# Fused attention and feed-forward layer on one core: slots of queries and keys copied on chip, and the last block's finish in halves with precedence

## The reference

```python
Q, K = apply_rope(Q), apply_rope(K)
attn = einsum('bqhd,bkhd->bhqk', Q, K) * head_dim ** -0.5      # causal mask, softmax
x = x + (attn @ V) @ w_proj + b_proj                           # on layernorm(x)
real = layernorm(x) @ cos(theta + theta_noise)
imag = layernorm(x) @ sin(phi + phi_noise)
x = x + sqrt(real * real + imag * imag)
```

## Time and profile before

| | |
|---|---|
| median of three runs | 2075.5 us (2075.34 to 2077.35) |
| the profiled execution | 2075.44 us, its span 2073.7 us, so 1.7 us lie outside the span |
| TensorE busy | 98% of the span |
| VectorE, ScalarE, GpSimd busy | 72%, 68%, 42% |
| mean granted TensorE clock | 0.992 of full speed |

### The profile page before, as it was taken

How to read it: one execution, slowest core, us unless ns; L and a number is a source line. 1 busy time by engine, 2 the same in 40 slices (tenths; PEclk the granted TensorE clock), 3 DMA queues, 4 the chain that set the end, 5 groups by cost and what they waited for, 6 DMA issues and landing times.

```text
span 2073.7 us, 39127 instructions
## 1 busy us (share of the span) xinstructions
PE 2028.7 (98%) x13124; PEld 877.2 (42%) x13124; DVE 1493.0 (72%) x2724; ACT 1403.4 (68%) x2705; POOL 871.7 (42%) x1336
## 2 busy tenths in 40 slices
PE   7999999999999999999999999999999999999988
PEld 5333343344443444444443444434444344433335
DVE  4858878877768777786767768787676877678423
ACT  2455667777667666776667676687666767677673
POOL 3334426353433435544263453447343353630252
PEclk9999999999999999999999999999999999999999
DMA  5322322232222322232222212333222232320031
GB/s 144 80 47 86 88 62 78 78 95 72 72 74 61 90 77 73 88 95 73 66 86 80 81 58 65 95 97 88 78 62 76 66 95 77 89 80 17 28 123 44
DMA packets 120552, 159.90 MB, mean 77 GB/s; under 512 B 30746, under 2 KB 82586, under 8 KB 120346
## 3 DMA queue, kind: packets, MB, share of 16 engines
q1 hardware_dynamic: 118480, 154.18, 25.4%
q10 hardware_dynamic: 1872, 3.21, 0.8%
HBM read 88.89 MB, written 50.85 MB: 67 GB/s over the span
## 4 chain that ended last, share of the span: by engine, by line
PE 83%; ACT 6%; issue 3%; DMA 3%; POOL 2%; DVE 2%; SPq 1%; ACTq 0%; DVEq 0%; POOLq 0%
PE banks L938 21%; PE banks L916 21%; PE banks L953 20%; PE banks L871 5%; PE banks L882 5%; ACT probs L1049 3%; PE banks L914 3%; PE banks L898 3%; PE banks L834 2%; DVE chunk_max L1195 1%; ACT inverse L1069 1%; ACT xin L1062 1%; PE banks L823 1%; DMA stack_k<-split 1%; POOL guess L1272 1%
## 5 line engine op out<-in xcount | busy, mean ns | idle before, releaser
L1195 DVE TENSOR_REDUCE chunk_max<-banks 128x1 f32<-128x512 f32 (+3 forms) x2240 | 1350.4, 667 | 393.6 <-PE banks L916 389.3
L1049 ACT ACTIVATE probs<-banks 128x512 f32<-128x512 f32 (+1 forms) x2240 | 1141.3, 601 | 384.7 <-PE banks L938 302.3
L916 PE MATMUL banks<-stack_k,stack_q 96*128 96x512 bf16 (+3 forms) x2560 | 730.5, 351 | 4.9 <-DVE chunk_max L1195 2.1
L938 PE MATMUL banks<-stack_q,stack_k 99*128 99x512 bf16 (+3 forms) x2560 | 695.1, 350 | 11.7 <-ACT probs L1049 9.2
L953 PE MATMUL banks<-probs,v_one 128*17 128x512 f32 (+3 forms) x5120 | 527.7, 532 | 4.2 <-POOL probs L1337 3.1
L938 PEld LDWEIGHTS banks<-stack_q,stack_k 99*128 99x128 bf16 x2560 | 231.9, 97 | 393.8 <-ACT probs L1049 206.4
L916 PEld LDWEIGHTS banks<-stack_k,stack_q 96*128 96x128 bf16 x2560 | 239.8, 98 | 240.4 <-DVE chunk_max L1195 75.7
L1337 POOL TENSOR_SCALAR_AFFINE_SELECT probs<-probs 128x512 f32<-128x512 f32 x256 | 160.7, 638 | 220.0 <-ACT probs L1049 219.5
L953 PEld LDWEIGHTS banks<-probs,v_one 128*17 128x17 f32 x5120 | 119.0, 96 | 288.6 <-issue 192.2
L914 PE MATMUL banks<-diag_mask,ident_bf 128*128 128x128 bf16 x1024 | 200.7, 223 | 6.2 <-DMA stack_k<-split 4.4
L587 POOL TENSOR_TENSOR turned<-raw,cos_t 128x512 f32<-128x512 f32 x62 | 78.9, 1273 | 290.7 <-ACT raw L1011 287.6
(11 more groups left out here) (134 smaller groups left out, 1181.2 us busy)
## 6 DMA issues: line engine op xcount, KB each, us to landing
split<-parts SPq DMA_DIRECT2D x64, 384.0 KB, 2.7
stack_q<-split SPq DMA_DIRECT2D x384, 64.0 KB, 2.2
stack_k<-split SPq DMA_DIRECT2D x354, 64.0 KB, 2.2
sums<-o_raw SPq DMA_DIRECT2D x64, 256.0 KB, 2.2
rot<-raw SPq DMA_DIRECT2D x246, 64.0 KB, 2.0
xin<-x SPq DMA_DIRECT2D x16, 512.0 KB, 4.0
heads_t<-sums SPq DMA_DIRECT2D x26, 256.0 KB
mid<-x SPq DMA_DIRECT2D x13, 512.0 KB, 4.0
```

What stands on the lines that cost most here:

```text
L916: mm = nc.tensor.matmul(bank[:, n * wide:(n + 1) * wide], stack_q[u % 2][0:SPLIT_ROWS, t, h + n, j * P:(j + 1) * P], stack_k[u % 2][0:SPLI ...
L938: mm = nc.tensor.matmul(bank[:, a * wide:(a + 1) * wide], stack_k[u % 2][0:ROWS, j // SUB, first + a, (j % SUB) * P:(j % SUB + 1) * P], st ...
L1049: nc.scalar.activation(probs[:, g % PROBS, first:first + many, w0:SPAN], bank, ACT.Exp).then_inc(s_exp, 1)
L1195: nc.vector.tensor_reduce(to, bank[:, 0:count * wide].rearrange("p (h n) -> p h n", h=count), AX.X, ALU.max).then_inc(s_emptied["DVE"], 1)
```

## The change

Three things are changed, and one number with them.

1. **Slots are read from `parts`.** `keep`, the DRAM tensor `split` and its semaphore go. Each slot copy reads 64 partitions of `parts`, 1 KB of each, where it read 16 rows of 4 KB from DRAM. `fetch` and `fetch_k` wait for the last rope instruction, and rope instruction 3, which writes `parts`, waits for the slots of two spans before (it waited for their `keep`; the `keep` itself waited for those slots).
2. **The last block.** `spread`, the reciprocal over a whole bank and the multiplication on `o_raw` give way to `apart` (four transposes that bring rows to partitions), a reciprocal of 16 numbers a partition, a multiplication out of the bank, `together` (four transposes back) and a copy. Its stats, deviation, apply and `xt3` go in halves. Every job of it has the due time `LAST_AT` = 15.4, ahead of the finishes of blocks 13 and 14.
3. **Block 14** has its power, modulus, add and final in halves too (`IN_HALVES`), on VectorE and ScalarE where GpSimd did them.
4. **Numbers of the plan:** `apply` 2.1 for 1.35 us, `exp` 0.02 us longer, the scores of the last span due 0.1 of a unit earlier.

```diff
 FINAL = BLOCKS - 1
+
+IN_HALVES = (FINAL - 1, FINAL)
+LAST_AT = 15.4
+LAST_PULL = 0.1
 SETS = SPANS
...
+
+    def halved(n, a, at):
+        job(("power", n, a), "DVE", 0.7, at, [("out", ("wave", n, 2 * a + 1))])
+        job(("modulus", n, a), "ACT", 0.6, at, [("power", n, a), ("modulus", n, a - 1)])
+        job(("add", n, a), "DVE", 0.7, at, [("modulus", n, a)])
+        job(("final", n, a), "SP", 0.4, at, [("add", n, a), ("final", n, a - 1)], 3.0)
...
         unit = GROUPS * b + GROUPS - 1
-        todo.append((GROUPS * (b + 1) + t + 0.1 if b < BATCH - 1 else ends(unit, t) + 0.05, "finish", n, 0))
+        todo.append((GROUPS * (b + 1) + t + 0.1 if b < BATCH - 1 else LAST_AT if n == FINAL else ends(unit, t) + 0.05, "finish", n, 0))
...
-            job(("apply", n), "ACT", 1.35, at, [("dev", n)])
+            job(("apply", n), "ACT", 2.1, at, [("dev", n)])
...
-                after += [("keep", *ago)] if n == 3 else []
+                after += [("fetch", *ago), ("fetch_k", *ago)] if n == 3 else []
...
-            job(("keep", u, c), "SP", 0.45, at, [("rope", u, c, ROPE_OPS - 1), ("fetch", *ago), ("fetch_k", *ago)], 2.4)
             if i < HELP:
-                job(("fetch_k", u, c), "ACT", 3.6, at, [("keep", u, c)], 2.2)
-            job(("fetch", u, c), "SP", 2.7 if i < HELP else 5.4, at, [("keep", u, c), ("scores", LAST_STEP.get(u - 2), 0)], 2.2)
+                job(("fetch_k", u, c), "ACT", 3.6, at, [("rope", u, c, ROPE_OPS - 1)], 2.2)
+            job(("fetch", u, c), "SP", 2.7 if i < HELP else 5.4, at, [("rope", u, c, ROPE_OPS - 1), ("scores", LAST_STEP.get(u - 2), 0)], 2.2)
...
-                job(("spread",), "PE", 0.85, at, [("lift", unit, t), ("lead", n, 1), ("weights",)])
-                with_bank(("spread",), ("spread",), "DVE", 3.6, at)
-                job(("divide",), "DVE", 0.7, at, [("out", ("spread",))])
+
+                at = LAST_AT
+                job(("apart",), "PE", 0.44, at, [("lift", unit, t), ("weights",)])
+                with_bank(("apart",), ("apart",), "DVE", 0.85, at)
+                job(("together",), "PE", 0.44, at, [("out", ("apart",))])
+                with_bank(("together",), ("together",), "DVE", 0.65, at)
                 for a in range(2):
...
+                    job(("proj", n, a), "PE", 0.9, at, [("out", ("together",)), ("lead", n, 1), ("proj", n, a - 1)])
+                    with_bank(("proj", n, a), ("proj", n, a), "DVE", 0.65, at, [("out", ("lead", n, a))])
+                    job(("stats3", n, a), "DVE", 1.0, at, [("out", ("proj", n, a)), ("stats3", n, a - 1)])
+                    job(("dev3", n, a), "POOL", 2.8, at, [("stats3", n, a), ("dev3", n, a - 1)])
+                    job(("apply3", n, a), "ACT", 1.05, at, [("dev3", n, a)])
+                    job(("xt3", n, a), "PE", 0.44, at, [("apply3", n, a), ("xt3", n, a - 1)])
+                    with_bank(("xt3", n, a), ("xt3", n, a), "ACT", 0.55, at)
+                    for j in (2 * a, 2 * a + 1):
+                        job(("wave", n, j), "PE", 4 * KT * 2 * DIM / 2400, at, [("out", ("xt3", n, a)), ("wave", n, j - 1)])
+                        with_bank(("wave", n, j), ("wave", n, j), "ACT", 0.6, at, [("power", n, 0)] if j > 1 else [])
+                    halved(n, a, at)
...
-                    job(("exp", g, n), "ACT", 0.06 + many * wide / 1200, at, [("scores", g, n), prev, ("values", g4 - g4 % VALUES)])
+                    job(("exp", g, n), "ACT", 0.08 + many * wide / 1200, at, [("scores", g, n), prev, ("values", g4 - g4 % VALUES)])
```

The addresses of the slot copies, the waits, and the new products:

```diff
-                    engine.wait_ge(s_keep[i % 2], 16 * (i // 2))
+                    engine.wait_ge(s_fetch[i % 2], LOADS * (i // 2))
...
             tile = (stack_q, stack_k)[side][u % 2][slot * HD:(slot + 1) * HD, c, :, :]
-            rows = split[PLACE[u, c] % 2, part, side * P // 2:(side + 1) * P // 2, :]
-            return tile.rearrange("p h n -> p (h n)"), rows.rearrange("(d h) n -> d (h n)", h=HG)
+            rows = parts[side * P // 2:(side + 1) * P // 2, PLACE[u, c] % 2, part, :]
+            return tile, rows
...
-                def keep_parts(u, c):
+                def fetch_slots(u, c):
                     i = PLACE[u, c]
                     sp.wait_ge(s_rope, ROPE_OPS * (i + 1))
-                    if i >= 2:
-                        sp.wait_ge(s_fetch[i % 2], LOADS * (i // 2))
-                    sp.dma_start(split[i % 2].rearrange("m r n -> r m n"), parts[:, i % 2, :, :]).then_inc(s_keep[i % 2], 16)
-
-                def fetch_slots(u, c):
-                    i = PLACE[u, c]
-                    sp.wait_ge(s_keep[i % 2], 16 * (i // 2 + 1))
                     if u >= 2:
                         sp.wait_ge(s_scores, FILLS[LAST_STEP[u - 2] + 1])
...
-                def spread_denominators():
+                def turn_sums():
                     u, t = SCORED[-1]
                     pe.wait_ge(s_lift, len(SCORED))
-                    pe.wait_ge(s_last_weights, 32)
-                    bank = bank_of(("spread",))
-                    nc.tensor.matmul(bank, spread, o_raw[:, TURN[u, t] % 2, :], start=True, stop=True).then_inc(s_filled["DVE"], 1)
+                    bank = bank_of(("apart",))
+                    for j in range(SUB):
+                        mm = nc.tensor.transpose(bank[:, j * P:(j + 1) * P], o_raw[:, TURN[u, t] % 2, j * P:(j + 1) * P], ident[:, :])
+                    mm.then_inc(s_filled["DVE"], 1)
+
+                def turn_back():
+                    emptied(pe, ("apart",))
+                    bank = bank_of(("together",))
+                    for j in range(SUB):
+                        mm = nc.tensor.transpose(bank[:, j * P:(j + 1) * P], last_rows[:, j * P:(j + 1) * P], ident[:, :])
+                    mm.then_inc(s_filled["DVE"], 1)
+
+                def turn_last(a):
+                    pe.wait_ge(s_last_norm, a + 1)
+                    bank = bank_of(("xt3", FINAL, a))
+                    for k in range(KT):
+                        for j in range(2):
+                            at = (2 * k + j) * P
+                            mm = nc.tensor.transpose(bank[:, at:at + P], normed3[finish_set(FINAL)][:, 2 * a + j, k * P:(k + 1) * P], ident[:, :])
+                    mm.then_inc(s_filled["ACT"], 1)
...
-                    pe.wait_ge(s_divided, 1)
+                    emptied(pe, ("together",))
+                    pe.wait_ge(s_last_weights, 16)
                     bank = bank_of(("proj", FINAL, a))
```

VectorE's part of it, and its norm statistics in halves (the new functions `deviation_last` and `normalise_last` do the same eight and two instructions on half of the columns):

```diff
+                def block_stats_last(a):
+                    emptied(dve, ("proj", FINAL, a))
+                    for j in (2 * a, 2 * a + 1):
+                        nc.vector.bn_stats(last_stats[:, j, :], mid[finish_set(FINAL)][:, j, :]).then_inc(s_last_stat, 1)
+                    dve.wait_ge(s_last_stat, 4 * a + 2)
+                    for j in (2 * a, 2 * a + 1):
+                        nc.vector.bn_aggr(last_mv[:, j, :], last_stats[:, j, :]).then_inc(s_last_stat, 1)
...
-                    if item[0] == "spread":
+                    if item[0] == "apart":
                         dve.wait_ge(s_rope, ROPE_OPS * len(PROJECTED))
-                        nc.vector.reciprocal(crossed[:, :], bank).then_inc(s_emptied["DVE"], 1)
+                        sums_of = bank.rearrange("p (j h v) -> p j h v", h=HG, v=VW)
+                        nc.vector.reciprocal(last_inverse, sums_of[:, :, :, HD]).then_inc(s_last_inverse, 1)
+                        dve.wait_ge(s_last_inverse, 1)
+                        inverse = last_inverse.unsqueeze(3).to_broadcast([P, SUB, HG, VW])
+                        nc.vector.tensor_tensor(last_rows.rearrange("p (j h v) -> p j h v", h=HG, v=VW), sums_of, inverse,
+                                                ALU.mult).then_inc(s_emptied["DVE"], 1)
+                        return
+                    if item[0] == "together":
+                        nc.vector.tensor_copy(last_heads[:, :], bank).then_inc(s_emptied["DVE"], 1)
```

More of the change, by code:

```diff
@@ L211, in plan @@
         job(("tables", c), "SP", 0.9, CLOCK[0, c - 1] - 1.05, [("rot", 0, c - 1)], 5.0)
-    job(("wv",), "SP", 0.8, -0.7, [("keep", 0, 0)], 3.0)
+    job(("wv",), "SP", 0.8, -0.7, [("rope", 0, 0, ROPE_OPS - 1)], 3.0)
     job(("wqk",), "SP", 0.5, -0.3, [("fetch", 0, 2)], 3.0)
@@ L513, in layer_kernel @@
         late_wproj = wqk[:, 0, :, :].rearrange("p k n -> p (k n)")
-        spread = wqk[:, 1, 0, :]
         last_heads = turned
+        last_rows = raw[:, 0, :]
+        small = iter(crossed[:, n * 4 * SUB:(n + 1) * 4 * SUB] for n in range(9))
+        last_stats = crossed[:, 256:256 + 6 * SUB].rearrange("p (j s) -> p j s", s=6)
+        last_inverse = next(small).rearrange("p (j h) -> p j h", h=HG)
+        last_mv = next(small)[:, 0:2 * SUB].rearrange("p (j s) -> p j s", s=2)
+        last_variance, last_centre, last_guess, last_correction, last_rstd, last_shift = (next(small)[:, 0:SUB] for _ in range(6))
         out_bank = psum[RING]
@@ L550, in layer_kernel @@
         s_rope = sem("rope_chain")
```

(28 more changed lines are left out.)

135 lines of the change are left out of this document (70 added, 65 removed).

## The result

The changed kernel takes 2051.07 us (median of 4 runs, 2046.19 to 2051.54) against 2075.42 of before in the same comparison: ratio 0.9876, 95% interval 0.9859 to 0.9893. The profiled execution took 2051.54 us, with a span of 2049.4.

A forecast was written before the change was run, and what follows sets the result against it. TensorE, busy 98% of the span, was taken as the bound, except at the opening and the end. From 2075.4 us, opening -4, body +4 and end -9.2 gave 2066.2 us, range 2056 to 2074.5.

The forecast's parts named there:

- The opening: Start of the kernel: earlier slots and new order of unit 0 gain 4 us, from a loss of 4 to a gain of 10.
- The second span: Opening: its slots, issued at about 36.4, reach TensorE at 44.5 to 45.4 against 49.82, a gain of 5 us.
- The third step, the hole: Opening, unit 0's order: VectorE's 16 us hole moves forward between maxima of spans 2 and 3, TensorE having about 16 us work.
- The slots' own price: Slot copies in 1 KB pieces out of SBUF: priced at nothing, at worst four times the time.
- The rule of the packet floor: Slot copies: about 10.5 ns per packet would add 2 us to each span's slots, 2072 in all; thought contradicted by 252 GB/s.
- The body: Middle, TensorE-bound: more changes between kinds of matmul lose 4 us, from a loss of 8 to a gain of 3.
- The prediction's two terms: Body: more changes between kinds cost 5.0 us, about 1 in the opening; better placement gains at most 15.4 us of idle.
- The end: Behind the last `lift`: fillers and waiting for block 15's norm go, 9.2 us less, from 6 to 10.
- The margins of 0.9 and 2.2 us: End: block 15's two normed halves are ready 0.9 and 2.2 us before TensorE needs them; an overrun loses time.
- the first, 2056: Rival, whole kernel: opening keeps 10 us, new order costs nothing, end gives 9.2; 2056 us, chance 0.16 (below 2061).

The follow-up runs named there:

- e4: Kernel before with its order kept, slot copies reading parts on chip without the store to DRAM: 2066.08 us, ratio 0.9962.
- e2: Changed kernel with the plan's exponential duration back at 0.06 us instead of 0.08: 2062.05 us, ratio 0.9937.
- e1: Kernel before with only the plan's exponential duration changed from 0.06 to 0.08 us: 2070.70 us, ratio 0.9978.
- e9: Changed kernel with the plan's exponential duration at 0.04 us instead of 0.08: 2065.74 us, ratio 0.9955.
- e10: Changed kernel with the plan's exponential duration at 0.082 us instead of 0.080: 2049.60 us, ratio 0.9883.
- e5: Changed kernel with the plan's exponential duration at 0.10 us instead of 0.08: 2049.03 us, ratio 0.9882.
- e7: Changed kernel with the first norm's `apply` duration in the plan back at 1.35 us from 2.1: 2055.27 us, ratio 0.9912.
- e11: Changed kernel with the plan's exponential at 0.10 us and VectorE's maximum at 0.085 instead of 0.07: 2044.19 us, ratio 0.9860.
- e12: Changed kernel with the plan's exponential at 0.10 us and VectorE's maximum at 0.100 instead of 0.07: 2051.91 us, ratio 0.9892.
- e6: Changed kernel with block 15's due time `LAST_AT` at 16.2 instead of 15.4, so without precedence: 2057.24 us, ratio 0.9927.
- e8: Changed kernel with block 14's power, modulus, add and final whole again on GpSimd: 2051.66 us, ratio 0.9899.

## Why the prediction was wrong

**The opening** was right in mechanism and a little short: -4 forecast, -6.7 measured. The first product was put at 33.0 and came at 33.91. The second span was put at 44.5 to 45.4 and came at 47.46, as its slots are issued at 38.15, not 36.4, and needed 9.3 us to the first product where 8.1 to 9 were allowed. The third step, the hole, came where it was put (94 to 113 instead of 140 to 156), with TensorE working 14.7 of 19 us, so it stands idle for 4.3 us there where it was 2.8 in the old hole; the slots of the fourth span, issued at 104.08, were used at 112.72. e4 keeps its 6.9 us with before's order, so the new order of unit 0 gains nothing over it, and in e2 the order takes all but 1.0 back. The slots' own price, taken as zero, was a little more: 8.6 us from issue to first product where the earlier trace rows have 8.1. The rule of the packet floor, from the Trainium skill, "DMA: Bandwidth & Descriptors", section "Measured (HBM→SBUF, 128 partitions, SWDGE, issued from GpSimd)", gave an estimate of 2 us more; the trace shows 0.5 on this other kind of DMA, so the rule did not bind here.

**The body** is where it failed. The step that failed reads: "longer ScalarE times in the plan ..., which may place products better; the 15.4 us of idle bound that gain. I take a loss of 4 us". Two things in it were wrong. First, idle is no bound of the waiting. The idle column fell from 15.4 to 11.0 us, while 11.8 us came off in this stretch. Records of matmuls hold their latency and overlap, so a start that is late by less than that shows no idle. A bf16 product of 512 columns shows a record of 0.38 us while the next one starts 0.21 behind it, so 0.17 us of lateness leave no trace in the idle column.

What the late starts cost can be summed. I took TensorE's list between the cuts at step 48 and step 600 from the start of each record to the start of the next, sorted these steps by the kinds and sizes of the two records, and took for each kind the tenth percentile over all profiles as its quick step. The quick steps add up to the list's own time, the rest is lateness (us; the two miss the stretch by up to 0.7, as a step across a cut is not shared out):

| kernel | to 600 | quick steps | lateness | of it ahead of scores |
|---|---|---|---|---|
| before | 1668.2 | 1601.3 | 66.5 | 32.3 |
| e4, before, direct slots | 1668.4 | 1601.3 | 66.7 | 32.3 |
| e1, before, exp 0.08 | 1659.2 | 1606.4 | 52.6 | 24.2 |
| after | 1656.4 | 1608.1 | 47.8 | 16.9 |
| e2, after, exp 0.06 | 1669.0 | 1601.8 | 67.0 | 21.1 |
| e9, after, exp 0.04 | 1673.2 | 1600.3 | 72.7 | 34.9 |
| e10, after, exp 0.082 | 1657.0 | 1608.2 | 48.4 | 19.4 |
| e5, after, exp 0.10 | 1656.7 | 1609.2 | 47.2 | 15.7 |
| e7, after, `apply` 1.35 | 1661.8 | 1606.9 | 54.5 | 19.5 |
| e11, e5 and max 0.085 | 1654.0 | 1610.8 | 42.9 | 12.4 |
| e12, e5 and max 0.100 | 1662.3 | 1611.5 | 50.6 | 15.9 |

With any share from the second percentile to the median the differences between the kernels stay within some 0.6 us, though the level of the lateness moves. The prediction's two terms stand side by side in it. The list did get longer, by 6.8 us, for the more frequent changes of kind that were priced at 5.0 (with 1 of it in the opening). The waiting fell by 18.7 us, of which 15.4 were ahead of scores, where the prediction saw at most the 15.4 us of idle, and took nothing. Between the same two cuts the idle column fell only from 11.2 to 5.1 us.

The page's part 4 gives a hint of it, but no more. Before, e2, and after:

```profile
PE 83%; ACT 6%; issue 3%; DMA 3%; POOL 2%; DVE 2%; SPq 1%; ACTq 0%; DVEq 0%; POOLq 0%
```

```profile
PE 80%; issue 6%; POOL 6%; ACT 3%; DVE 2%; DMA 2%; SPq 1%; ACTq 0%; DVEq 0%; POOLq 0%
```

```profile
PE 88%; POOL 3%; DMA 3%; issue 2%; ACT 2%; DVE 2%; SPq 0%; ACTq 0%; DVEq 0%; POOLq 0%
```

TensorE is busy 98% in before and after, but only 83% of before's chain runs through it. The share does not rank the runs, though: e1 has 82% and is 9.0 us faster in the body than before, e9 has 87% and the slowest body. The chain of before at 914 us shows one place of lateness: an `apply` of 2.08 us, planned as 1.35, stands between exponentials, and the next score waits for the exponential behind it. The idle column has 0.66 us of that.

```profile
914.54 1.08 ACT xin L1062 x2
915.62 0.49 ACT probs L1049
916.10 0.04 issue
916.15 0.39 PE banks L938
```

Second, I priced the exponential's 0.02 us as nothing. That this number makes the difference is shown, both ways, by e1, e2, e9 and e10, and the table shows where it lands: in TensorE's late starts, about half of them ahead of scores in before and e9, a third in e2. Why a number above ScalarE's pace is worth more than one at the pace is not shown. A candidate that no run tried: from an exponential's end to the start of the next one out of the same bank the plan allows 0.34 us and the score's columns (0.13 + 0.01 + 0.2), while in the profile after the commonest value, from the end of one record to the start of the other and without the columns, is 0.6 to 0.7 (269 of 1739 cases in steps 24 to 599). The plan's trip through a bank would then be too short, and slack in the exponential's number would make up for part of it.

**The stretch before the last `lift`** was in no step: 3.6 us lost. TensorE waits 3.97 us there for the multiplication of block 14's heads, where it waited 2.34 before. The multiplication itself waits for the inverses' trip through DRAM (7.57 us of VectorE's idle time, 7.31 before). All of TensorE's idle time in this stretch is 12.7 us, against 9.3. The clock is not the cause: its lower level is granted for 10.2 us of this stretch in both profiles. It does fall at this place: the granted share is 0.62 between 2007 and 2011 us, the mean of a stretch partly at 1.2 and partly at 2.4 GHz, and the 16 matmuls of `proj` take 5.41 us. But they took 5.41 us in before too, and 3.72 where the clock stayed up (e4, e6). Before, after, e4, e6 and e8, the same 16 matmuls:

```profile
2021.79 5.41 PE L834 MATMUL banks<-wproj,stack_q 128*128 128x256 f32 x16 [2.34 <-DVE stack_q L1151]
```

```profile
2006.95 5.41 PE L849 MATMUL banks<-wproj,stack_q 128*128 128x256 f32 x16 [3.97 <-DVE stack_q L1200]
```

```profile
2017.04 3.72 PE L827 MATMUL banks<-wproj,stack_q 128*128 128x256 f32 x16 [3.58 <-DVE stack_q L1144]
```

```profile
2005.90 3.72 PE L849 MATMUL banks<-wproj,stack_q 128*128 128x256 f32 x16 [2.74 <-DVE stack_q L1200]
```

```profile
2006.96 6.36 PE L849 MATMUL banks<-wproj,stack_q 128*128 128x256 f32 x16 [3.36 <-DVE stack_q L1200]
```

**The end** was right: -9.2 forecast, -9.4 measured. `apart`'s reciprocal took 0.26 us (0.24 forecast), the last wave ended 29.8 us behind `lift` (30), the span 35.5 (36), and TensorE did not wait for the halves: their transposes stand at 2028.91 and 2034.50 with no gap. The margins of 0.9 and 2.2 us held.

Of the rivals the first, 2056, had the sign of the miss: the order costs nothing. Even it left the body's gain out.

## What to carry to other kernels

Where a plan written ahead sets the order, try its durations, one at a time and both ways: 20 ns on an instruction that runs 2240 times were worth 9.0 and 12.6 us of the body here, more than the data path. Do not take such a duration from a row of the trace divided by its count; the distance from start to start is the pace. And do not take for granted that the true pace is the best number. Do not bound the waiting of a pipelined engine by its idle column; compare the starts of its records with the quickest step of the same kind. And before counting a DMA that is removed, see whether the bounding engine ever waits for it: with the order held fixed, 25 MB less of traffic moved nothing outside the opening.

## What the runs showed of the hardware

- Copies of 64 KB from 64 partitions in 1 KB pieces landed 2.6 us behind their issue where those out of DRAM in 4 KB pieces took 2.2, and six of them took 4.07 us to issue on ScalarE's queue where the earlier trace rows have 2.73.
- Exponentials of 512 columns out of a bank start 0.478 us apart (median, before and after) while each record lasts about 0.60, and maxima of 512 columns on VectorE start 0.598 apart.
- The length of a wait did not tell whether the clock would fall behind it. Behind 2.34 us (before), 3.97 (after) and 3.36 (e8) the 16 matmuls of block 14's `proj` took 5.41, 5.41 and 6.36 us, behind 2.74 (e6) and 3.58 (e4) they took 3.72. Before and e4 have the same order on every engine, but for the store.
